# A decoder layer on one core: the attention stage reordered, with att one batch behind, and a rounding in two vector operations

## The reference

```python
Xn = layernorm(X) * gamma + beta
Q, K, V = split(Xn @ W_in + b_in)              # (4, 512, 512) each
K, V = rotary(K), rotary(V)                    # on the first 256 features
A = sum over tokens of K/|K| * V/|V|           # one row of 512 for a batch
Y = (0.5 * A + 0.5)[:, None, :] * Q
x = layernorm(X + (Y @ W_out + b_out + X))     # attention stage
x = layernorm(x + fp8_round(x) @ fp8_round(ctx) + mask)     # cross stage
x = layernorm(x + silu(x @ gate_w) * (x @ up_w) @ down_w + experts(x))
```

## Time and profile before

| | us |
|---|---|
| runs | 910.62, 907.69, 906.86 (median 907.69) |
| profiled execution, its own time | 910.76 |
| its span in the profile | 909.0 |
| PE busy | 821.1 (90%) |
| PEld busy | 665.0 (73%) |
| DVE busy | 715.6 (79%) |
| POOL busy | 412.4 (45%) |
| ACT busy | 268.3 (30%) |

### The profile page before, as it was taken

One profiled execution on the slowest core, in us unless ns is written; L12 is line 12 of the kernel. 1 busy time (PEld: TensorE's weight loads), 2 busy tenths in 40 slices (PEclk: granted clock), 3 DMA queues, 4 the chain that ended last, 5 costly groups with the idle time before them and its releaser, 6 DMA issues. The chain is left out here.

```text
span 909.0 us, 11100 instructions
## 1 busy us (share of the span) xinstructions
PE 821.1 (90%) x3746; PEld 665.0 (73%) x3750; DVE 715.6 (79%) x1376; ACT 268.3 (30%) x615; POOL 412.4 (45%) x310
## 2 busy tenths in 40 slices
PE   2999999999962598889999999999999999999995
PEld 2787877878750376568888888888887887787784
DVE  4697845647368989941677799999999999999997
ACT  2222230322302331222123543342343342333330
POOL 3122161341404441412124777677567667676431
PEclk9999999999985599999999999999999999999998
DMA  4822010010153321220000223232233332331113
GB/s 153 332 94 93 1 47 0 0 46 1 48 184 116 83 66 28 70 93 23 1 29 27 74 85 86 73 85 74 75 91 99 90 94 75 112 103 55 48 47 138
DMA packets 45652, 69.08 MB, mean 76 GB/s; under 512 B 17215, under 2 KB 26175, under 8 KB 45088
## 3 DMA queue, kind: packets, MB, share of 16 engines
q1 hardware_dynamic: 27168, 49.63, 16.3%
q0 software_dynamic: 18432, 18.80, 7.9%
HBM read 108.34 MB, written 12.58 MB: 133 GB/s over the span
## 5 line engine op out<-in xcount | busy, mean ns | idle before, releaser
L928 POOL TENSOR_TENSOR h_lo<-mid,h_hi 128x512 fp32r<-128x512 f32 x62 | 79.4, 1302 | 123.4 <-ACT h_hi L1046 119.0
L949 POOL DMA_INDIRECT ctx_q<-table_dram,row_i x64 | 80.4, 1257 | 62.2 <-DVE xall L1278 42.6
L1384 PE MATMUL gu<-x_hi,gate_hi 128*128 128x512 f32 x256 | 102.9, 402 | 3.1 <-DVE mid L1178 1.7
L1385 PE MATMUL gu<-x_lo,gate_hi 128*128 128x512 f32 x256 | 101.0, 395 | 0.0
L1386 PE MATMUL gu<-x_hi,gate_lo 128*128 128x512 f32 x256 | 100.7, 393 | 0.0
L949 POOL DMA_INDIRECT scratch<-table_dram,row_i x64 | 82.7, 1292 | 39.5 <-issue 21.3
L1385 PE MATMUL gu<-x_lo,up_hi 128*128 128x512 f32 x256 | 99.6, 389 | 0.0
L1384 PE MATMUL gu<-x_hi,up_hi 128*128 128x512 f32 x256 | 99.6, 389 | 0.0
L1386 PE MATMUL gu<-x_hi,up_lo 128*128 128x512 f32 x256 | 99.6, 389 | 0.0
L1384 PE MATMUL ob<-down_hi,h_hi 128*128 128x512 f32 x248 | 97.3, 392 | 1.0 <-POOL h_lo L928 1.0
L1056 ACT ACTIVATE gates<-dots 128x1 f32<-128x1 f32 x144 | 29.3, 203 | 232.0 <-DVE dots L1269 232.0
(11 more groups left out here) (199 smaller groups left out, 1801.2 us busy)
## 6 DMA issues: line engine op xcount, KB each, us to landing
stage<-in_ctx SPq DMA_DIRECT2D x8, 1024.0 KB, 5.4
xall<-in_x SPq DMA_DIRECT2D x4, 1024.0 KB, 9.1
w_stage<-in_L_ffn_gate_w SPq DMA_DIRECT2D x8, 512.0 KB, 3.7
w_stage<-in_L_ffn_up_w SPq DMA_DIRECT2D x8, 512.0 KB, 3.3
w_stage<-in_L_ffn_down_w SPq DMA_DIRECT2D x8, 512.0 KB, 3.5
x_dram<-xall SPq DMA_DIRECT2D x4, 1024.0 KB, 4.9
x_tok<-x_dram SPq DMA_DIRECT2D x16, 256.0 KB, 3.2
out<-xall SPq DMA_DIRECT2D x8, 512.0 KB, 2.6
```

Of the source, the lines that this page charges most:

```text
L928: nc.gpsimd.tensor_tensor(lo[:, c], mid[c][:], hi[:, c].bitcast(F32), ALU.subtract).then_inc(hlo_done, 1)
L949: nc.gpsimd.indirect_dma_start(rows[k], None, table_dram[:, :], bass.IndirectOffsetOnAxis(ap=row_i[t % 2][:, k:k + 1], axis=0), bounds_che ...
L1384: nc.tensor.matmul(dst, lhs[0], rhs[0], start=start, stop=False)
L1385: nc.tensor.matmul(dst, lhs[0], rhs[1], start=False, stop=False)
```

## The change

1. *Weights and gamma/beta.* W_in's key/value columns come in four chunks of 512 KB, each with its own half of a staging buffer, so all four are in flight from the beginning; the query columns are one later DMA of 1 MB into `qT`. gamma and beta are no longer folded into the weights: ACT applies them as scale and bias when it takes the transposed x out of PSUM (`xs`), and a second ACT pass makes the high part. The bias products and the operations around them go. x's first half is loaded by SP and its second half by ACT's queue.
2. *Transposes by chunk.* `transposes(b, c)` makes chunk c for all four tiles of a batch, so `xhat` holds four tiles; `high` and `low` go chunk by chunk. In batch 0, `key_value` of tiles 0 and 1 is interleaved by chunk.
3. *att one batch behind.* PE's list for a batch b from 1 on ends with the att product of b - 1; the last batch's att product stands alone at the end. The mix matmuls of b - 1 stand behind `key_value(b, 1)`, `y_hi` and `y_lo` of b - 1 are made in the middle of batch b, and the last batch's `y` lies in the `xn` tiles. `residual` of b - 1 is followed by its statistics, and `finish_x1` of b - 2 begins batch b. For the last batch, variance, power and `finish_x1` go tile by tile.
4. *token sums* of a tile stay on PE, two tiles behind its `key_value`; their copy `rsum` goes from DVE to ACT.
5. *Rounding in two operations.* ACT makes m = |y| x (2^20 - 2^11) as bf16 (Abs), and DVE does y = max(m, c) + y and x_q = max(m, c) - y, for the context (now on DVE and ACT alone) and for x. Constants and signs differ accordingly; the order in which the context's batches are rounded is 3, 0, 1, 2.
6. The loops over batches 1 and 2 are written out.

```diff
@@ sync
-                def load_w(c):
-                    if c >= 2:
-                        sp.wait_ge(w_hi_done, c - 1)
-                        sp.wait_ge(w_lo_done, c - 1)
-                        sp.wait_ge(bias_mm, c - 1)
-                    sp.dma_start(stage[c % 2][:, 0:3 * D], w_in_v[c]).then_inc(w_raw[c], 16)
+                sp.dma_start(xall[:, 0:2 * D], x_tiles[0][:, 0]).then_inc(x_half, 16)
+                sp.dma_start(ident[:], consts[:, C_ID:C_ID + P]).then_inc(ident_in, 16)
+                for c in range(KC):
+                    sp.dma_start(w_stage_of(c), w_in_v[c][:, D:3 * D]).then_inc(w_raw[c], 16)
+                ...
+                sp.dma_start(qT[:], w_in.rearrange("(c p) n -> p c n", p=P)[:, :, 0:D]).then_inc(wq_raw, 16)
+                load_x(1)
@@ scalar
-                    nc.scalar.activation(w_hi[:, c, :], stage[c % 2][:, 0:3 * D], ACT.Copy, scale=gam[:, c:c + 1]).then_inc(w_hi_done, 1)
+                    nc.scalar.activation(w_hi[:, c, D:3 * D], w_stage_of(c), ACT.Copy).then_inc(w_hi_done, 1)
+                def high(b, c):
+                    ...
+                    nc.scalar.activation(xs[:, c % 2], ob[c % 2][:], ACT.Identity, scale=gam[:, c:c + 1], bias=bet[:, c:c + 1]).then_inc(xs_done, 1)
+                    act.wait_ge(xs_done, j + 1)
+                    ...
+                    nc.scalar.activation(xn_hi[:, c], xs[:, c % 2], ACT.Copy).then_inc(hi_done, 1)
+                def ctx_scale(n):
+                    ...
+                    nc.scalar.activation(stage[1][:], stage[1][:], ACT.Copy, scale=scale_c[:, 0:1]).then_inc(c_scaled, 1)
+                    act.wait_ge(c_scaled, n + 1)
+                    nc.scalar.activation(stage[0][:].bitcast(BF16)[:, 0:KC * D], stage[1][:], ACT.Abs, scale=ROUND_TO_4_BITS).then_inc(c_y, 1)
@@ vector, a batch
+                for b in range(B):
+                    if b == 1:
+                        dve.wait_ge(c_amax, B)
+                        largest(amax_c[:])
+                    if b == 3:
+                        ctx_quantise(2)
+                    if b >= 2:
+                        for i in range(TB):
+                            finish_x1(b - 2, i)
+                    add_kv_bias(b, 0)
+                    if b == 1:
+                        scale_row(0)
+                    if b < LAST:
+                        next_stats(b + 1)
+                    if b == 0:
+                        low_wq()
+                    if b == 1:
+                        scale_all(scale_c, 0)
+                    add_kv_bias(b, 1)
+                    products(b, 0)
+                    if b:
+                        multiplier(b - 1)
+                        for c in range(KC):
+                            low_y(b - 1, c)
+                    else:
+                        low_wo()
+                        ctx_amax(0)
+                    if b < LAST:
+                        normalise(b + 1)
+                    add_kv_bias(b, 2)
+                    products(b, 1)
+                    ...
+                    add_kv_bias(b, 3)
+                    products(b, 2)
+                    ...
+                    products(b, 3)
+                    ...
+                    if b < LAST:
+                        low(b + 1, 0)
+                        low(b + 1, 1)
+                    if b:
+                        residual(b - 1, 0)
+                    ...
+                finish_x1(2, 0)
+                finish_x1(2, 1)
+                residual(LAST, 0)
+                variance((0,))
+                ...
@@ tensor, a batch
+                for b in range(B):
+                    if b:
+                        for k in range(KC):
+                            key_value(b, 0, k)
+                        if b == 1:
+                            gather_largest(0)
+                        for k in range(KC):
+                            key_value(b, 1, k)
+                        if b == 1:
+                            spread(0)
+                            pe.wait_ge(scale_done, 1)
+                        mix_sums(b - 1)
+                    for i in (2, 3):
+                        for k in range(KC):
+                            key_value(b, i, k)
+                        token_sums(b, i - 2)
+                    for c in range(KC):
+                        query(b, c)
+                        if c in (1, 2):
+                            token_sums(b, c + 1)
+                    if b < LAST:
+                        transposes(b + 1, 0)
+                        transposes(b + 1, 1)
+                    if b == 1:
+                        pe.wait_ge(wo_lo_done, 1)
+                    if b:
+                        attention(b - 1, 0, b)
+                    if b < LAST:
+                        transposes(b + 1, 2)
+                        transposes(b + 1, 3)
+                    if b:
+                        attention(b - 1, 1, b)
+                        if b == LAST:
+                            mix_sums(LAST)
+                        attention(b - 1, 2, b)
+                        attention(b - 1, 3, b)
+                for i in range(TB):
+                    attention(LAST, i, None)
@@ cross stage, scalar and vector
-                        nc.scalar.activation(y_q[i], gu[i][:], ACT.Copy, scale=scale_x[:, 0:1]).then_inc(y_done, 1)
+                        nc.scalar.activation(y_q[i], gu[i][:], ACT.Copy, scale=scale_x[:, 0:1]).then_inc(y_scaled, 1)
+                        act.wait_ge(y_scaled, j + 1)
+                        nc.scalar.activation(m_q[i], y_q[i], ACT.Abs, scale=ROUND_TO_4_BITS).then_inc(y_done, 1)
-                        own.did(nc.vector.tensor_scalar(m.bitcast(U32), y.bitcast(U32), EXPONENT_BITS, None, ALU.bitwise_and))
+                        own.did(nc.vector.scalar_tensor_tensor(y, m, ROUND_SUBNORMAL, y, ALU.max, ALU.add))
                         own.wait()
-                        own.did(nc.vector.tensor_scalar(m, m, FP8_MIN_NORMAL, ROUND_TO_4_BITS, ALU.max, ALU.mult))
-                        own.wait()
-                        own.did(nc.vector.tensor_tensor(y, y, m, ALU.add))
-                        own.wait()
-                        nc.vector.tensor_tensor(x_q[:, i].rearrange("p c n -> p (c n)"), y, m, ALU.subtract).then_inc(q_done, 1)
+                        nc.vector.scalar_tensor_tensor(x_q[:, i].rearrange("p c n -> p (c n)"), m, ROUND_SUBNORMAL, y, ALU.max, ALU.subtract).then_inc(q_done, 1)
```

More of the change, by code:

```diff
@@ new lines, in squares @@
+                def squares(b, i):
+                    j = TB * b + i
+                    act.wait_ge(kv_out, j + 1)
+                    if j >= 2:
+                        act.wait_ge(wgt_ready, j - 1)
+                    for which in range(2):
+                        if j or which:
+                            act.wait_ge(sq_done, 2 * j + which)
+                        nc.scalar.activation(junk[:], kv[:, i % 2, which], ACT.Square, accum_out=norm2[:, i % 2, which:which + 1]).then_inc(sq_done, 1)
@@ L389, in _ @@
+                for c in range(KC):
+                    high_y(LAST, c)
             @block.vector
@@ new lines, in next_stats, with normalise @@
+                def next_stats(b):
+                    dve.wait_ge(x_in[b], 16)
+                    own.wait()
+                    x_stats(b, range(TB))
+                    x_variance(b)
+                def normalise(b):
+                    dve.wait_ge(rstd_ready, b + 1)
+                    if b:
+                        dve.wait_ge(xt_mm, KC * b)
+                    for i in range(TB):
+                        j = TB * b + i
+                        nc.vector.tensor_scalar(xhat[:, i], tile(j), mv[:, j, 0:1], rstd[:, j:j + 1], ALU.subtract, ALU.mult).then_inc(xhat_done, 1)
@@ new lines, in finish_x1 @@
+                def finish_x1(b, i):
+                    j = TB * b + i
+                    if b == LAST:
+                        dve.wait_ge(rstd2_ready, LAST + i + 1)
+                    else:
+                        dve.wait_ge(rstd2_ready, b + 1)
+                    own.did(nc.vector.tensor_scalar(tile(j), tile(j), mv2[:, i, 0:1], rstd2[:, i:i + 1], ALU.subtract, ALU.mult))
+                    own.wait()
+                    nc.vector.tensor_reduce(amax_x[:, j:j + 1], tile(j), AX.X, ALU.max, apply_absolute_value=True).then_inc(x1_done, 1)
```

689 lines of the change are left out of this document (328 added, 361 removed).

## The result

The changed kernel takes 881.5 us (median of 4 runs, 875.9 to 883.0) beside 908.9 us for the kernel before: a ratio of 0.969, 95% interval 0.964 to 0.974. The prediction was 884, its range 864 to 902. In a second series of six runs the median was 882.4 (876.5 to 884.4). The profiled execution read here took 880.46 us with a span of 878.6, so it stands against the span of 909.0 before: 30.4 us less.

What follows compares the result with a forecast made beforehand. TensorE, busy 90% of the span, was the bound, with time lost at the start, in attention waits, the tail and VectorE's rounding. 15 - 2 + 3.5 + 8 = 24.5 us off 907.7 gave 883.2, stated as 884, range 864 to 902.

Steps and rivals of the forecast that it cites:

- 1, start: Up to the first key/value matmul: first product at 15.3 us instead of 32.3, gain 15 us after 2 of slow clock.
- 2, att behind: Attention stage: 13.2 us of waits and slow clock removed, 15.0 us of new waits; worth about -2 us.
- the scale: Attention stage, batch 1: PE waits 0.8 us for the scale.
- token_sums(1) of batch 0: Attention stage: VectorE needs 11.7 us from products(0) to products(1), so PE waits 4.3 us, plus a 1.7 us slow stretch.
- 3, tail: From last att matmul to maximum of x: finishing tile by tile gains 3.2 us, 3.5 with one operation less in `largest`.
- T + 9.8: VectorE's tail schedule ends 9.8 us after the last att matmul, T, against 13.0 before.
- 4, rounding: Second stage: two rounding operations gain 5 us in the first four tiles and 3 in later periods, 8 in all.
- a gain in two periods, 3 for both: Later second-stage periods: net 0.2 to 2.2 us each in two periods, ScalarE's lateness counted; 3 us taken for both.
- C: Rival: VectorE becomes the attention stage's bound, waits double, each with a slow stretch; +15, 899 us; chance 0.17.
- B: Rival: 8 of 15 us of new waits vanish and the second stage gives 13 instead of 8; 871 us; chance 0.22.
- E: Rival: Abs between Copies in `scaled` and `ctx_scale` makes ScalarE reload its table; 925 us; chance 0.05.
- D: Rival: the second stage waits for its table loads and hands back the earlier gain; 902 to 907 us; chance 0.04.

Runs made afterwards that it cites:

- experiment 1: The changed kernel with x's old rounding: four operations on VectorE again, no Abs on ScalarE; 891.4 us, ratio 0.981.
- experiment 3: The changed kernel with two key/value weight chunks in flight instead of four; 882.8 us, ratio 0.972.
- experiment 4: The changed kernel with att, `y` and its residual back in the batch they belong to; 882.5 us, ratio 0.970.
- experiment 6: The changed kernel with VectorE's order altered in batch 2 alone, 879.9 us; in batch 0 as well, 870.1; with late Abs too, 867.2.
- the run with batch 2 alone: The changed kernel with VectorE's order altered in batch 2 only: next batch's normalisation behind products(1), context's rounding behind products(2); 879.9 us, ratio 0.968.
- experiment 2: The kernel before with only x's rounding in two operations on VectorE and the Abs pass on ScalarE; 895.7 us, ratio 0.986.
- the order mended: The changed kernel with VectorE's order altered in batches 2 and 0, context maxima started early between other work; 870.1 us, ratio 0.958.

## Why the prediction was right, point by point

- **Sum.** Predicted 24.5 us; measured 30.4 by the spans and 27.4 by the medians. Start 15 against 14.8; att behind -2 against -3.4; tail 3.5 against 6.4 to 6.6; rounding 8 against 12.4, of which experiment 1 gives 10.6 to the rounding itself. What was missing is in two terms, both sized too small, the tail and the rounding. That the start and att came out so near is in part luck, as the next two points show.
- **1, start.** Right in its chain, with a smaller slow-clock loss (1.4 for 2) and a wait for beta (1.56) that was not in it. That four chunks in flight matter is only weakly borne out (experiment 3).
- **2, att behind.** The net was near, the parts were not. Of the predicted waits, batch 0's token_sums(0) (3.4 against 4.2), batch 2's (2.1 against 2.1), the transposes of batch 1 (1.7 against 1.25; a third wait of that line, 0.6, is at the start), the scale (0.8 against 0.3) and batch 3's (1.0 against 0.9) are there. Both waits for products came with 1.9 to 2.2 us of VectorE operations slowed beside POOL, which the prediction had at nothing to speak of. token_sums(1) of batch 0 (4.3) is not there: the operations named for it add to 10.0 us and not to 11.7, they took 9.2, and PE, at half clock, came 3.4 us later. Missing from the list were 1.9 us for the residual ahead of the last tiles; and the slow clock costs 6.8 us (the two long stretches at half the rate) where I had counted 1.7. The step "by the earlier trace rows a gap of this size brings a slow stretch, 1.7" was mis-sized: with one-column matmuls behind the gap a stretch costs 3.4. And the credit of 7.7 us to the shift is not the shift's: the kernel with att in its own batch waits 0.3 (experiment 4), and its trace points to the wait by chunk and the faster `y_lo`, neither of which the prediction counted.
- **3, tail.** "T + 9.8" was T + 6.6. The direction was right. From the variance of the third batch to the maximum VectorE took 17.7 us where the hand schedule has 19.4. The other 1.5 us are no gain: the last att matmul itself is 1.9 us late because PE waited for residuals, the same time that point 2 lacks. Tile by tile gives 2 to 3 us by itself (the run with the tail grouped).
- **4, rounding.** First four tiles 4.3 for 5; ScalarE's lateness 3.36 for 3.2. The step that was mis-sized is "a gain in two periods, 3 for both". From the first variance to the second `x_lo` nothing was gained but 1.35 us lost (34.5 to 35.8); the next period gave 3.0, more than the 0.2 to 2.2 worked out; the last, before which ScalarE has no cross products to scale, went from 28.5 us to 23.5; and 1.4 us came behind it. That is 8.1 us for 3. Abs and Copy for four tiles cost 5.2 us, predicted 5.6. On the blocked operations: above the 0.69 us that the same form takes alone, the two operations lost 4.5 us in the first four tiles (2 x 1.48 + 2 x 0.78), beside 6.8 before: 3.0 by the earlier trace rows, and 3.8 of the other three operations (means of 931, 930 and 604 ns, in four, four and five times, where 430, 690 and 430 are usual). The Trainium skill, "SBUF — State Buffer", section "SBUF: two separate sides", says that a VectorE operation with two SBUF inputs and one of GpSimd that reads SBUF exclude each other for a whole instruction; by half as many operations half the loss should have gone. The trace shows a third gone: fewer operations, each blocked longer (up to 2.71 us).
- **Rivals.** C was right about its place (waits for VectorE's products, each with a slow stretch), but it happened twice and not in every batch, and experiment 6 shows that order and not VectorE's load was the cause: the same work in another order takes 12 us less. B was half right: the second stage gave 12.4 for its 13, and the period of 27.0 is the sign it had named (well under 28), but of the waits of the attention stage little went. E is refuted: no table load at Abs, with 16 Abs operations among the Copies of the cross stage. There the Trainium skill, "ScalarE: Activation LUTs", section "Table sets: the hidden batching unit", agrees with the trace. D did not occur: the 18.0 us won up to the cross stage are whole in the end.

What stays open: why a row of one-column matmuls brings a stretch at one place and not at another, and in one run 3.4 and in another 7 us, was not settled. Nor was it measured what PE loses to the VectorE operations that are slow beside POOL.

## What to carry to other kernels

Before an operation on a shared engine is moved back because nobody waits for it, list what it covers: a load in flight may need exactly that filler. When a wait vanishes in a bundle of edits, undo the edit that was meant to remove it; here the wait stayed away, and another edit, down to how many chunks a wait asks for, has to be looked for. And if a kernel's own runs spread by 1% on one core, compare their granted clocks before averaging them.

## What was not expected of the hardware

Eight one-column products in a row (16 passes, 1.84 us at full clock) can stand ahead of a stretch at 1.2 GHz with no wait of PE near them: about 3.4 us of it behind the row at 141.66 us in the run with batch 2 alone, and behind the one at 229.75 in the run with att in its own batch. Most rows have none behind them: of the sixteen in the first profile of the changed kernel only the two that follow a wait. A wait of 2.1 or 4.2 us, in one run 1.75, followed by such a row had about 7 us behind it; waits of 2.0 to 2.3 us followed by dense matmuls had 3.4 us in the kernel before. But one and the same wait (1.98 us, the second batch) had a stretch behind it in the profile of the kernel before and none in that of experiment 2, so neither the wait nor the row settles it. With the products spread out between dense matmuls the one profile taken has no stretch.

The changed kernel spreads over 7.9 us from run to run and with the order mended over 2.8. That the two long stretches make the spread is not shown: the kernels of experiments 1 and 3 and the one with the tail grouped have both of them and spread over 3.0 to 3.3.
